# Chunk and step loops of three graph layers written out, and two VectorE operands read from PSUM

## The reference

```
x = x + L0(relu(layernorm(x)), ...)       # gated messages from an edge MLP, summed per target
x = x + L1(relu(layernorm(x)), W, att)    # attention, 4 heads
x = x + L2(relu(layernorm(x)), ...)       # agg[dst] += weight * (x @ w_nbr)[src];  + x @ w_own + bias
x = x + L3(relu(layernorm(x)), ...)       # attention, 8 heads, then a feed-forward and two batch norms

# an attention layer, per edge and head:
e     = leaky_relu(es[src] + ed[dst])
m     = segment_max(e, dst);  ex = exp(e - m[dst])
out   = segment_sum(ex / segment_sum(ex, dst)[dst] * z[src], dst)
```

## Time and profile before

| | us |
|---|---|
| median of 3 runs | 8612.5 |
| profiled execution | 8678.63 |
| its span | 8676.9 |
| layer 0 (edges), about 610 to 2900 | 2290 |
| layer 1 (edges), about 3055 to 4585 | 1530 |
| layer 2 (edges), about 4790 to 6090 | 1300 |
| layer 3 (edges), about 6400 to 8045 | 1645 |

### The profile page before, as it was taken

The page is one execution under the profiler, slowest core; times in us unless marked ns, Lnnn a source line. Parts: engine busy times, 40 slices in busy tenths (PEclk is TensorE's granted clock), DMA queues, the critical chain, the costliest instruction groups (busy, mean ns, idle before and its releaser), DMA issues. The chain is left out here.

```text
span 8676.9 us, 128745 instructions
## 1 busy us (share of the span) xinstructions
PE 5902.0 (68%) x29234; PEld 4310.6 (50%) x29235; DVE 5168.6 (60%) x12724; ACT 1984.6 (23%) x6402; POOL 3831.7 (44%) x4450
## 2 busy tenths in 40 slices
PE   2289999999999645555556555555845555555864
PEld 1178888888888533333334333333323333333553
DVE  4757777777776445665664444444326666777445
ACT  1045555555554311111112000000111111111232
POOL 1013333333333066666660666666026656675000
PEclk7589999999999867777778666666967767777587
DMA  2121111111111333333321233333033323232200
GB/s 76 43 81 53 51 51 53 51 51 53 51 52 50 114 96 89 85 87 83 86 73 58 86 90 90 90 90 89 28 92 85 82 74 82 79 89 67 62 6 31
DMA packets 319334, 606.56 MB, mean 70 GB/s; under 512 B 92201, under 2 KB 195565, under 8 KB 318719
## 3 DMA queue, kind: packets, MB, share of 16 engines
q0 software_dynamic: 171200, 474.81, 19.8%
q1 hardware_dynamic: 140746, 123.45, 4.7%
q10 hardware_dynamic: 7200, 6.56, 0.2%
HBM read 548.80 MB, written 62.98 MB: 71 GB/s over the span
## 5 line engine op out<-in xcount | busy, mean ns | idle before, releaser
L288 POOL DMA_INDIRECT G<-table,ib x1760 | 1917.2, 1089 | 470.5 <-issue 470.5
L186 POOL DMA_INDIRECT G<-table,ib x1760 | 1684.1, 957 | 470.2 <-issue 470.2
L560 PE MATMUL pM<-G,one 128*128 128x260 f32 (+1 forms) x3520 | 1282.1, 485 | 603.5 <-issue 212.1
L215 DVE TENSOR_TENSOR acc<-acc,pM 128x512 f32 (+1 forms) x1760 | 967.1, 549 | 600.2 <-DMA xr<-x 292.0
L560 PEld LDWEIGHTS pM<-G,one 128*128 128x128 f32 x3520 | 651.8, 221 | 1092.6 <-DVE acc L425 547.8
L425 DVE TENSOR_TENSOR acc<-acc,pM 128x260 f32 (+1 forms) x1760 | 758.0, 431 | 670.6 <-PE pM L560 391.7
L638 PE MATMUL pM<-G,one 128*128 128x256 f32 x1760 | 702.3, 550 | 592.3 <-DVE one L628 405.7
L1278 ACT ACTIVATE oh<-one,a4S 128x128 f32<-128x128 f32 x2640 | 861.6, 389 | 1.1 <-issue 0.9
L638 PEld LDWEIGHTS pM<-G,one 128*128 128x128 f32 x1760 | 427.2, 267 | 867.4 <-DVE one L628 462.1
L1357 PE MATMUL pM<-prod,oh 128*128 128x64 f32 x3520 | 681.9, 275 | 0.0
L479 ACT ACTIVATE oneT<-pT 128x512 bf16<-128x512 f32 x440 | 261.8, 597 | 1771.3 <-PE pT L544 893.9
(11 more groups left out here) (309 smaller groups left out, 8619.1 us busy)
## 6 DMA issues: line engine op xcount, KB each, us to landing
G<-table,ib POOLq DMA_INDIRECT x3520
far<-step_rec SPq DMA_DIRECT2D x224, 64.0 KB
table<-row SPq DMA_DIRECT2D x100, 128.0 KB
table<-row SPq DMA_DIRECT2D x50, 132.0 KB
table<-row SPq DMA_DIRECT2D x50, 130.0 KB
base<-aux SPq DMA_DIRECT2D x50, 128.0 KB
bs<-base SPq DMA_DIRECT2D x50, 128.0 KB
x<-xo ACTq DMA_DIRECT2D x50, 128.0 KB
```

The costliest lines, as they stand in the source:

```text
L186: pool.indirect_dma_start(G[j][:, :], None, rows, bass.IndirectOffsetOnAxis(ap=ib[:, j:j + 1], axis=0)).then_inc(s_g[j], 16)
L215: nc.vector.tensor_tensor(at, at, pM[j % R][:, :], ALU.add).then_inc(s_acc, 1)
L288: pool.indirect_dma_start(G[:, par * C + j, 0:ROW], None, tab, bass.IndirectOffsetOnAxis(ap=ib[:, par * C + j:par * C + j + 1], axis=0)).t ...
L560: nc.tensor.matmul(pM[j % R][:, :], one[:, par * C + j, :], G[:, par * C + j, :], start=True, stop=True).then_inc(s_m, 1)
```

## The change

Three things are changed.

1. `over_chunks` is a plain loop of the program's generator: all 29 rounds are straight code on each of the five engines, and all counts that were computed in registers are constants. `steps` does the same for layer 2 (unroll 16) and keeps the loop of layer 0 (unroll 8). The numbers of the node tiles are still loaded into registers.
2. `weigh` reads the weights from `pX` in PSUM in place of SBUF. Since they lie there in groups of four heads, it is one instruction in layer 1 as before, and two instructions of half the size in layer 3. The copy at L516 stays.
3. The counting row that `mark` compares with is copied once into PSUM (`pI`, in the bank of `pF`) and read from there. Marks 6 and 7 of a chunk now come before `factors`, together with 3 to 5.

```diff
-            with eng.Fori(peel, count // unroll) as i:
-                turn(i, False)
+            if peel < count // unroll:
+                with eng.Fori(peel, count // unroll) as i:
+                    turn(i, False)
...
-            pipelined(eng, K, u, 1, *parts)
+            pipelined(eng, K, u, 1 if u == U else K // u, *parts)
...
-                pF = se.ps("pF", [P, H])
+                pF = se.ps("pF", [P, P + H])
+                pI = pF[:, H:H + P]
...
-                    for a_ in range(3):
-                        do(a_, a_ % 2, C, C if a_ else 0)
-                    with eng.Fori(1, (NC - 2) // 2) as i:
-                        for r_ in (1, 2):
-                            do(2 * i + r_, r_ % 2, C, C)
-                    for a_ in range(NC - 1, NC + 1):
-                        do(a_, a_ % 2, TAIL if a_ < NC else 0, C if a_ < NC else TAIL)
+                    for a_ in range(NC + 1):
+                        do(a_, a_ % 2, C if a_ < NC - 1 else TAIL if a_ < NC else 0, 0 if a_ == 0 else TAIL if a_ == NC else C)
...
-                                                    iota[:, :].unsqueeze(1).broadcast_to([P, 4, P]),
+                                                    pI.unsqueeze(1).broadcast_to([P, 4, P]),
...
-                            rows_ = G[:, par * C + 4 * q:par * C + 4 * q + 4, :]
-                            z = rows_[:, :, 0:D].rearrange("p s (h c) -> p s h c", h=H)
-                            nc.vector.tensor_tensor(z, z, rows_[:, :, D:D + H].unsqueeze(3).broadcast_to([P, 4, H, D // H]), ALU.mult).then_inc(s_msg, 1)
+                            for g in range(GR):
+                                F = D // H
+                                z = G[:, par * C + 4 * q:par * C + 4 * q + 4, 4 * g * F:4 * (g + 1) * F].rearrange("p s (h c) -> p s h c", h=4)
+                                w = pX[:, g * P:(g + 1) * P].rearrange("p (h k) -> p k h", h=4)[:, 4 * q:4 * q + 4, :]
+                                ins = nc.vector.tensor_tensor(z, z, w.unsqueeze(3).broadcast_to([P, 4, 4, F]), ALU.mult)
+                            ins.then_inc(s_msg, 1)
...
+                        nc.vector.tensor_copy(pI, iota[:, :]).then_inc(s_z, 1)
...
-                            for q in range(3, min(6, mq)):
+                            for q in range(3, mq):
                                 mark(a_, par, q)
                             if n_b:
                                 nodes_of(b_, 0)
                                 factors(b_, 1 - par)
-                            for q in range(6, mq):
-                                mark(a_, par, q)
```

More of the change, by code:

```diff
@@ L401, in rescale @@
                             dve.wait_ge(s_f, b_ + 1)
-                            nc.vector.tensor_scalar(fS[:, :], pF[:, :], 1.0, None, ALU.add).then_inc(s_rs, 1)
+                            nc.vector.tensor_scalar(fS[:, :], pF[:, 0:H], 1.0, None, ALU.add).then_inc(s_rs, 1)
                             dve.wait_ge(s_rs, 3 * b_ + 1)
@@ L438, in _ @@
                         link(nc.vector.tensor_copy(part[:, :, 2, :], rest))
-                        dve.wait_ge(s_z, 2)
+                        nc.vector.tensor_copy(pI, iota[:, :]).then_inc(s_z, 1)
+                        dve.wait_ge(s_z, 3)
                         dve.wait_ge(s_rows, 32)
@@ L592, in chunk @@
                                 pe.wait_ge(s_R, b_ + 1)
-                                nc.tensor.matmul(pF[:, :], Lh[:, :], Rk[:, :], start=True, stop=True).then_inc(s_f, 1)
+                                nc.tensor.matmul(pF[:, 0:H], Lh[:, :], Rk[:, :], start=True, stop=True).then_inc(s_f, 1)
                             for q in range(C4):
```

## The result

The changed kernel took 9006.0 us (median of 4, 8996 to 9023) against 8623.8 (4 runs, 8588 to 8643): 1.045 times, interval [1.041, 1.049]. The forecast was 8280 in 8010 to 8540. The profiled execution took 9023.1, its span is 9021.3, 344 us above that of before. Later runs fell on several chips, of two kinds that the kernel before tells apart: on one it takes 8,601 to 8,624 us (medians), on the other 8,077 to 8,089. The two times above are of the first kind, called *late* here, the other *timely*. On a timely one the changed kernel took 7935.3 against 8080.7: 0.981 [0.978, 0.984]. So the sign of the change depends on the kind of chip, and this document has to explain both. The kind need not be permanent: the record gives number 3 to the late chip of experiments 1 to 4, and 35 minutes later to a timely one of experiment 6.

The account below looks back on a forecast made before the run. Neither POOL (45.5 us a chunk) nor the VectorE-TensorE-ScalarE chain (43.9) set layer 1's pace; late hand-offs did. Layer gains 146 + 162 + 27 = 335 us off 8678.6 gave 8344, less 66 over the median: 8280, in 8010 to 8540.

Parts of the forecast that it names:

- Contention between VectorE and POOL: Layers 1 and 3: VectorE stops slowing POOL's gathers; 4.2 us a chunk off POOL, bounds 0 and 4.2.
- The price of PSUM: VectorE's marks and weighings: reading one operand from PSUM costs 0, bounds 0 and 71 us.
- The weighing in two: Layer 3: two half-size weighings cost VectorE 0.5 us a chunk more.
- Marks 6 and 7: Layers 1 and 3: moving them ahead of factors fills an existing VectorE wait, costing nothing; bounds 0 to 65 us.
- late hand-offs: TensorE results reaching waiting engines late; taken to stay, as in layer 2, at 3.1 us a chunk over the chain.
- Straight code: Layers 1 to 3 lose loop branches; fetching code costs 0; layer 2 gains 27 us, bounds 0 and 162.
- rival D: All engines: straight code arrives late through the code queues, costing 380 us against 335 saved: 8660 us; chance 0.06.
- The pace that results: Chunk periods become 47.0 us in layer 1 (from 52.4) and 50.5 in layer 3 (from 56.5), gaining 146 and 162 us.
- Rival C: Layers 1 and 3: weighings no longer slow POOL, so more late hand-offs; 300 us lost, 8910 us; chance 0.08.
- Rival A: Layers 1 to 3: hand-offs come on time, chunks reach 43.9 and 47.4 us; 637 us gained, 7980; chance 0.22.
- Rivals B: Layers 1 and 3: POOL gains nothing from the operands; 154 us saved in all, 8460 us; chance 0.12.
- E: Whole kernel: gains cancel with costs, so nothing moves; 8570 to 8650 us; chance 0.07.

Follow-up runs that it names:

- experiment 1: Kernel before, loops kept, with weights and counting row read from PSUM and marks 6 and 7 moved; late chip: 9158.3 us against 8621.3, 1.063.
- experiment 2: Changed kernel with its straight code, but both operands read from SBUF again; late chip: 8434.0 us against 8621.3 for the kernel before, 0.979.
- experiments 3: Kernel before, loops kept, with only the weights read from PSUM; late chip: 9126.7 us against 8621.3, 1.059.
- experiment 4: Changed kernel plus a small product POOL waits for behind each gather of layers 1 and 3; late chip: 8496.8 us against 8621.3 for the kernel before, 0.985.
- experiment 6: Timely chip, against the kernel before: changed kernel 0.981, the same with SBUF operands 0.997, the same with POOL delayed behind every fourth gather 0.988.
- experiment 7: Changed kernel with short gathered rows in layer 1 and POOL delayed behind every fourth gather in layer 3; late chip: 8881.9 us against 8600.8 before, 1.034.

## Why the prediction was wrong

**Contention between VectorE and POOL: right.** 1089 to 956 ns, where 960 was named. The inference in the Trainium skill (SBUF — State Buffer, Who interferes with whom), that a VectorE instruction with two SBUF inputs would not hold up a gather, is refuted for these instructions: in experiment 6, on one chip and with nothing else changed, the gathers take 1145 ns with both operands in SBUF and 964 in the changed kernel.

**The price of PSUM: right at 0.** The weighing 1215 ns (1220 before), the mark 679 (685), each with an operand from PSUM. The 65 ns more that the Trainium skill's fixed costs give (VectorE: DVE Perf Modes, TRN2 errata) don't show.

**The weighing in two: right**, small: layer 3 is 0.3 us a chunk longer than with one instruction (48.1 and 47.8, timely chip), 0.5 forecast; the 0.3 hold all that the operands cost there.

**Marks 6 and 7: 0 was wrong, within the bounds.** VectorE's wait ahead of the rescale in layer 1 fell from 53.4 to 36.4 us, but the 53.4 hold ten late hand-offs (43.0 us) and don't measure the move. Experiments 3 and 1 do: loops and weights are alike, and the second has the moved marks (and the counting row in PSUM). The wait for `pF` in layer 1, in that order:

```profile
DVE fS L402 <- PE pF L596: 1.6, 3, 0.7
...
DVE fS L403 <- PE pF L596: 18.4, 27, 0.7
```

In layer 3 it is 1.0 and 27.2 us. TensorE was mostly ready (in experiment 1 it waits for VectorE's factors in 26 of 27 chunks), so the wait that the two marks used to fill is now open: 0.6 us a chunk in layer 1 and 1.0 in layer 3, some 43 us of VectorE's time of the 65 that were the bound. What that cost in the total was not measured by itself.

**Straight code: cost right at 0, gain larger than thought and of another kind.** 96 and 157 code packets came, and the "issue" idle of TensorE (201.9 us in layer 1) looks like rival D. It isn't: on the timely chip the same code has no such row among TensorE's waits in layer 1. Layer 2 gained 20 us, 27 were forecast. Straight code with operands in SBUF is worth 2.1% of the kernel on the late chip and 0.3% on a timely one: so what it takes away on the late one should mostly be late hand-offs and not branches, by the difference of the two.

**The pace that results: wrong.** This is the step that failed: "plus late hand-offs, which I have no reason to see vanish", taken at 3.1 us over the chain. They did not stay, they grew: 57.7 - 42 = 15.7 us a chunk in layer 1. Layer 3 came out at 63.8 where 50.5 was forecast. The profile of before held the reason. Its clean chunks are those with fewer and longer gathers. POOL's gathers in the clean straight chunk from 3230.1 (42.0 us) and in the late one from 3603.6 (62.6 us), each by busy time and mean and then by first and last start:

```profile
L288 POOL DMA_INDIRECT G<-table,ib x28 | 33.9, 1211 | 7.5 <-issue 7.5
L288 POOL DMA_INDIRECT G<-table,ib x28: 942/982/1883, 3229.7 to 3272.0; - x28
...
L288 POOL DMA_INDIRECT G<-table,ib x44 | 46.4, 1055 | 11.7 <-issue 11.7
L288 POOL DMA_INDIRECT G<-table,ib x44: 942/947/1879, 3603.5 to 3665.0; - x44
```

From start to start that is 42.3 / 27 = 1.57 us, the pace of experiment 4, against 61.5 / 43 = 1.43. The clean chunks of the loop, as the one around, hold a pause of POOL of some 12 us besides. These rows alone don't say what causes what; experiments 3 and 4 do. I booked the stretch under a weighing (6.87 us for four in place of 5.16) as a loss on POOL alone. Rival C named exactly this ("removes the brake"), put its point of decision at a layer-1 period over 52.4 and its price at 8910; the runs gave 57.7 and 9006. I gave it 0.08 on the argument that "POOL is soon two chunks ahead and must then pause". It does pause, 445.6 us in layer 1 in place of 195.4 (the 184.9 of the earlier trace rows end at 4400 us, before the layer does), and its pauses do end a late stretch. In layer 1 of the changed kernel's trace 114 adds start within a pause of POOL of over 3 us, and only 5 of them waited over 1.5 us, all in the first 2.7 us of the pause. But a pause ends as scatters free rows, and the next such wait ends 10.5 us after that at the earliest, most often within 15: so short a stretch of gathers back to back suffices for late hand-offs to return.

**Rival A, on the other kind of chip.** With hand-offs on time I had 43.9, 47.4 and 7980 us. The timely chip gave 42.3, 48.1 and 7935. Near as this is, 1.6 us less in layer 1 and 0.7 more in layer 3 cancel in part, and the 7980 was meant for the chip on which the kernel before took 8612. That it came so near is in part luck. What I could not see in one trace is that the lateness belongs to the chip as it was then.

**Rivals B, D and E** are out: gathers did speed up, the same code runs without loss on a timely chip, and the time moved by far more than E's 1%, with PSUM free and the moved marks at 43 us or less.

Open: by what mechanism issuing gathers delays TensorE's signals. The runs exclude straight code, VectorE's operands as such (experiment 4 keeps them in PSUM) and the amount of data (experiment 7). They don't tell POOL's issuing from the number of row transfers, since short rows are as many, nor a late signal from a product that ends late. Nor do they tell whether a chip is of a kind for good, what makes it one, or whether the signals missing from late traces have to do with it. The loss is there without the profiler too: the three other executions behind the 9006 took 8996 to 9008, the profiled one 9023. One version was measured that is faster than the kernel before on both kinds: straight code with SBUF operands (0.979 and 0.997). On timely chips the changed kernel is the best of those that compute the whole result (0.981); on late ones it is slower than the kernel before (1.045).

## What to carry to other kernels

A slowdown that one engine causes another may be what keeps a third on time: before you remove contention, look at which stretches of the trace are clean, and whether the contention lies in them. Where signals in a trace come late with no cause in the program, treat their share as something that grows with the pace of what surrounds them, give the case in which it grows a real chance, and price it from the worst chunks shown. Measure such a change on more than one chip.

## What the runs showed of the hardware

On a late chip an add of layer 1 waited up to 7.6 us for TensorE while POOL issued a gather each 1.28 us outside its pauses, and at most 0.6 with one each 1.56 to 1.6. Gathers at 1133 ns in the mean don't prevent it: experiment 2 has a wait of 9.0 us. On timely chips no add of layer 1 waited over 0.6 us at any pace that was tried: 1.28 us a gather, 1.37 and 1.45, and bursts of 16. In layer 2, whose parts are the same in both runs, POOL waits on the late chip and hardly at all on the timely one (late first):

```profile
POOL gate L186 <- ACT ib L163: 137.7, 47, 3.9
```

```profile
POOL gate L186 <- ACT ib L163: 0.3, 1, 0.3
```

Sixteen steps take 1263.8 and 1119.4 us / 55 = 23.0 and 20.4 us there. The clock isn't what makes the hand-offs late. Layer 2 (5000 to 5600 us), late and timely:

```profile
5000.00:5600.00 600.00, 337.45 (x842) 187.18 (x842) 279.48 (x842) 21.57 (x105) 419.46 (x523) 0.67 0.32 92
```

```profile
5000.00:5600.00 600.00, 523.36 (x942) 227.07 (x942) 324.67 (x942) 24.22 (x118) 472.62 (x590) 0.55 0.36 104
```

TensorE had the higher mean clock, 0.67, on the late chip, with 337 us busy of 600; on the timely one it was busy for 523 at 0.55, mostly the lower level, and still did 942 matmul instructions where the late chip did 842. In layer 1 it is the other way round, 0.68 on the late chip (the second row of experiment 7) against 0.81 on the timely one:

```profile
3150.00:4250.00 1100.00, 745.17 (x3425) 475.06 (x3423) 861.72 (x1920) 153.24 (x336) 830.23 (x1033) 0.81 0.40 109
```

The products of the scatter take 521 ns in the mean there on the late chip and 453 on the timely one, 64 x 0.068 = 4.4 us a chunk of the 57.7 - 42.3 = 15.4. So the lower clock can be a part of the loss of layer 1, but not a wait of 3.5 or 7.6 us for a product that took 1.24 at most in the place shown.
